# Target attention over a history of 200 tokens: the TensorE program as a loop of 96 batches, softmax and context per pair of groups

## The reference

```python
def _L0_rec_ref(target_item, history_sequence, mask, W_q, W_k, W_v, W_o):
    q = (target_item @ W_q).reshape(b, H, HD)
    k = (history_sequence @ W_k).reshape(b, S, H, HD)
    v = (history_sequence @ W_v).reshape(b, S, H, HD)
    scores = jnp.einsum('bhd,bshd->bhs', q, k) / SCALE
    scores = jnp.where(mask[:, None, :] == 0, NEG, scores)
    attn = jax.nn.softmax(scores, axis=-1)
    out = jnp.einsum('bhs,bshd->bhd', attn, v).reshape(b, A)
    return out @ W_o
```

## Time and profile before

| | us |
|---|---|
| median of 3 runs | 885.77 (878.54 to 888.96) |
| the profiled execution | 875.22 |
| its span | 873.4 |

### The profile page before, as it was taken

How to read it: one execution, slowest core, us unless ns; L and a number is a source line. 1 busy time by engine, 2 the same in 40 slices (tenths; PEclk the granted TensorE clock), 3 DMA queues, 4 the chain that set the end, 5 groups by cost and what they waited for, 6 DMA issues and landing times.

```text
span 873.4 us, 43392 instructions
## 1 busy us (share of the span) xinstructions
PE 598.9 (69%) x20451; PEld 442.2 (51%) x20451; DVE 507.5 (58%) x385; ACT 284.6 (33%) x971; POOL 27.2 (3%) x62
## 2 busy tenths in 40 slices
PE   4567667667667686667776677776676767757675
PEld 2345445446445464545554555554554545545454
DVE  4945567555665547575455774657565465774630
ACT  2312333233342233431333323333431333333233
POOL 2000000000000000000000000000000000000000
PEclk9998998998888888797988988989879897998987
DMA  8956677576876657787566885758785577875700
GB/s 351 415 173 248 273 279 311 181 274 229 309 276 223 257 219 290 277 296 271 198 246 264 307 309 190 294 203 310 277 310 223 203 263 276 312 288 204 287 17 6
DMA packets 45042, 221.42 MB, mean 254 GB/s; under 512 B 5184, under 2 KB 11840, under 8 KB 44864
## 3 DMA queue, kind: packets, MB, share of 16 engines
q1 hardware_dynamic: 44352, 217.60, 65.4%
q0 software_dynamic: 512, 1.05, 0.3%
HBM read 217.58 MB, written 1.05 MB: 250 GB/s over the span
## 4 chain that ended last, share of the span: by engine, by line
PE 54%; issue 21%; ACT 10%; DMA 9%; DVE 4%; POOL 1%; SPq 0%; ACTq 0%; DVEq 0%; POOLq 0%
PE ps_c L279 27%; PE ps_s L246 23%; DMA out<-out_sb 8%; ACT p_pad L389 6%; ACT probs L379 3%; DVE blocks L452 3%; PE ps_m L304 1%; PE ps_y L294 1%; DMA w_in<-L_rec_W_o 1%; ACT ctx_t L408 1%; PE ps_p L261 1%; POOL neg_score L188 1%; DVE probs_t L469 1%; PE ps_y L311 0%; PE ps_u L220 0%
## 5 line engine op out<-in xcount | busy, mean ns | idle before, releaser
L452 DVE STREAM_TRANSPOSE blocks<-hist 128x1664 f32<-128x1664 f32 (+1 forms) x256 | 452.3, 1814 | 224.6 <-PE ps_s L246 217.7
L279 PE MATMUL ps_c<-hist,p_pad 64*32 64x128 f32 x12800 | 251.2, 301 | 145.9 <-issue 109.5
L279 PEld LDWEIGHTS ps_c<-hist,p_pad 64*32 64x32 f32 x12800 | 211.6, 116 | 187.1 <-issue 144.6
L246 PE MATMUL ps_s<-blocks,u_pad 128*32 128x200 f32 x4096 | 248.8, 395 | 30.9 <-DVE blocks L452 22.1
L246 PEld LDWEIGHTS ps_s<-blocks,u_pad 128*32 128x32 f32 x4096 | 145.3, 129 | 111.9 <-DVE blocks L452 33.0
L389 ACT ACTIVATE p_pad<-ps_p,own 128x192 f32<-128x192 f32 (+1 forms) x512 | 166.3, 480 | 33.0 <-PE ps_p L261 33.0
L397 ACT COPY inv_ctx<-ps_y 128x2 f32<-128x2 f32 x32 | 5.1, 160 | 334.4 <-PE ps_y L294 334.4
L261 PE MATMUL ps_p<-probs_t,place_sel 128*32 128x112 f32 x1024 | 37.9, 298 | 70.5 <-DVE probs_t L469 70.5
L461 DVE COPY_PREDICATED neg_score<-mask,ps_s 128x400 f32<-128x400 int32 x32 | 19.6, 614 | 105.7 <-PE ps_s L246 105.7
L261 PEld LDWEIGHTS ps_p<-probs_t,place_sel 128*32 128x32 f32 x1024 | 28.1, 123 | 78.1 <-DVE probs_t L469 78.1
L408 ACT COPY ctx_t<-ps_m 128x128 f32<-128x128 f32 x64 | 19.1, 399 | 90.2 <-PE ps_m L304 90.2
(11 more groups left out here) (44 smaller groups left out, 98.2 us busy)
## 6 DMA issues: line engine op xcount, KB each, us to landing
hist<-r_history_sequence SPq DMA_DIRECT2D x128, 832.0 KB, 8.3
hist<-r_history_sequence SPq DMA_DIRECT2D x128, 768.0 KB, 10.1
mask<-r_mask SPq DMA_DIRECT2D x32, 200.0 KB, 8.5
x_sb<-r_target_item SPq DMA_DIRECT2D x16, 64.0 KB, 4.2
out<-out_sb POOLq DMA_DIRECT2D x16, 64.0 KB, 5.6
w_in<-L_rec_W_q SPq DMA_DIRECT2D x1, 64.0 KB, 1.9
w_in<-L_rec_W_k SPq DMA_DIRECT2D x1, 64.0 KB, 2.0
w_in<-L_rec_W_v SPq DMA_DIRECT2D x1, 64.0 KB, 8.2
```

The lines of the kernel that those rows point to most:

```text
L246: mm = pe.matmul(ps_s[s % 2][Q * b:Q * b + Q, i1 * S:(i1 + 1) * S].rearrange("p (t j) -> p t j", j=J), u_pad[s % 2][:, i, b, c, :], blocks ...
L279: mm = pe.matmul(ps_c[alpha][Q * i:Q * i + Q, 0:D], p_pad[rows, t, i, :], hist[(s * GROUPS + i) % SLOTS][rows, t, :], start=(t == 0), stop ...
L452: dve.transpose(blocks[g % 2][:, t0:t1].rearrange("p t c k -> p (t c k)"), hist[g % SLOTS][:, t0:t1, :].rearrange("p t d -> p (t d)"),).th ...
```

## The change

The unit of softmax and context is now a pair of groups, 32 batches; there are NP = 64 pairs, and a round is RING = 3 pairs, 96 batches, so 22 rounds, the last of one pair. PE runs pairs 1 to 60 as a hardware loop of 20 passes over three steps (`pe.Fori`); its waits in the loop compare with values computed from the loop's register. The other engines stay straight code. So that every pass uses the same buffers, `hist` has 6 slots instead of 10, and `u_pad`, `p_pad`, `ps_s`, masks and sums have three each; `blocks` has three instead of two, `neg_score` two.

With two groups only, `context` gives the other two column tiles to the tokens of other parity; `turn_context` multiplies by `par_sel`, which adds the two parts and transposes at once, into `ps_y`. `place` is 8 matmuls of 64 columns per pair instead of 16 of 32 per super. `combine` is 4 matmuls over 96 batches, ACT copies the result (`copy_combined`), and a new `replicate` of 4 matmuls per pair with the selection `rep_sel` puts it where ACT spreads it from. `expand` is one set of 8 activations for all 25 tokens. The copy of the context is a function of its own (`copy_context`), after `spread`, and the stores come once in three pairs. SP loads w_v and w_o one group earlier, and a mask per pair, 800 bytes a row where a super's had 1600. The host permutes the mask to match, as before for its layout.

The removed functions are those printed above. Of the diff, cut (lines that are only "..." mark what is left out):

```diff
-    GROUPS = 4
-    SUPER = GROUP * GROUPS
-    NS = B // SUPER
-    NG = NS * GROUPS
-    ROUND = 2 * SUPER
-    NR = B // ROUND
-    SLOTS = 10
-    HALVES = ((0, 13), (13, T))
+    PAIR = 2 * GROUP
+    NP = B // PAIR
+    RING = 3
+    SLOTS = 2 * RING
+    ROUND = RING * PAIR
+    NR = (NP + RING - 1) // RING
+    BLOCKS = 3
+    HALVES = ((0, 12), (12, T))
     TQ = 7
     NEG = 1e9
     INV_SCALE = float(HD) ** -0.5
-    assert D == P and GROUP * J == P and S == T * J and B % ROUND == 0 and GROUPS == 4
+    LOOPS = (NP - 1) // RING - 1
+    assert D == P and GROUP * J == P and S == T * J and NP == RING * (LOOPS + 1) + 1
...
+        blocks = [sb(f"blocks{n}", [P, T, 4, Q]) for n in range(BLOCKS)]
+
+        u_pad = [sb(f"u_pad{n}", [P, 2, B4, 4, Q]) for n in range(RING)]
+
+        p_pad = [sb(f"p_pad{n}", [P, T, 2, Q]) for n in range(RING)]
...
+            for p in range(NP):
+                for i in range(2):
+                    g = 2 * p + i
+                    for h, (t0, t1) in enumerate(HALVES):
+
+                        wait(sp, ctx_done, 2 * (p - RING) + h + 1)
+                        sp.dma_start(
+                            hist[g % SLOTS][:, t0:t1, :], history_v[g * P:(g + 1) * P, t0:t1, :],
+                        ).then_inc(hist_loaded[g % SLOTS][h], 16)
+                    if i == 0:
+                        wait(sp, masked, p - RING + 1)
+                        rows = mask[p * Q:(p + 1) * Q, :]
+                        sp.dma_start(mask_sb[p % RING][:, :],
+                                     rows.unsqueeze(1).broadcast_to([Q, H, S])).then_inc(mask_loaded[p % RING], 16)
+                    if p == 0 and i == 0:
+                        for n, w in ((2, w_v), (3, w_o)):
+                            sp.dma_start(w_in[:, n, :], w).then_inc(vo_loaded, 16)
...
+            for p in range(2, NP):
+                pool.wait_ge(exp_done, p - 1)
+                pool.memset(neg_score[p % 2][:, :], NEG).then_inc(filled, 1)
...
+            def combine(r):
+                pe.wait_ge(x_t_copied, r + 1)
+                for h in range(H):
+                    mm = pe.matmul(ps_u[:, h * ROUND:(h + 1) * ROUND], w_qk[:, h, :], x_t[:, :],
+                                   start=True, stop=True)
+                mm.then_inc(u_done, 1)
+
+            def replicate(p, ring, r):
+
+                pe.wait_ge(u_copied, r + 1)
+                wait(pe, u_pad_ready, p)
+                for c in range(4):
+                    mm = pe.matmul(
+                        ps_u[:, :].rearrange("p (n c h) -> p c h n", c=4, h=H)[:, c],
+                        rep_sel[:, c].rearrange("p a d -> p (a d)"),
+                        u_sb[:, :, ring * PAIR:(ring + 1) * PAIR], start=True, stop=True)
+                mm.then_inc(u_rep_done, 1)
+
+            def scores(p, ring, i):
+                pe.wait_ge(turned, 4 * p + 2 * i + 2)
+                if i == 0:
+                    pe.wait_ge(u_pad_ready, p + 1)
+                slot = (2 * ring + i) % BLOCKS
+                for c in range(4):
+                    for b in range(B4):
+                        mm = pe.matmul(
+                            ps_s[ring][Q * b:Q * b + Q, 0:S].rearrange("p (t j) -> p t j", j=J),
+                            u_pad[ring][:, i, b, c, :],
+                            blocks[slot][:, :, c, J * b:J * b + J],
+                            start=(i == 0 and c == 0), stop=(i == 1 and c == 3),
+                        )
...
+            def place(q):
+
+                pe.wait_ge(probs_turned, q + 1)
+                wait(pe, expanded, q)
+                for x in range(4):
+                    for alpha in range(2):
+                        mm = pe.matmul(
+                            ps_p[64 * alpha:64 * alpha + 64, 0:4 * TQ * 16].rearrange(
+                                "p (q x i r) -> p x q i r", q=TQ, x=4, i=2)[:, x],
+                            place_sel[:, x].rearrange("p l b j -> p (l b j)"),
+                            probs_t[:, :, :].rearrange("p q (i l r) -> p l q i r", i=2, l=2)[:, alpha],
+                            start=True, stop=True,
+                        )
+                mm.then_inc(placed, 1)
+
+            def context(ring, half):
+                t0, t1 = HALVES[half]
+                for t in range(t0, t1, 2):
+                    for alpha in range(2):
+                        rows = slice(64 * alpha, 64 * alpha + 64)
+                        for i in range(2):
+                            for par in range(min(2, t1 - t)):
+                                at = Q * (2 * i + par)
+                                mm = pe.matmul(
+                                    ps_c[alpha][at:at + Q, 0:D],
+                                    p_pad[ring][rows, t + par, i, :],
+                                    hist[2 * ring + i][rows, t + par, :],
+                                    start=(t == 0), stop=(t + par + 2 >= T),
+                                )
+                mm.then_inc(ctx_done, 1)
...
+            def turn_context():
+                for alpha in range(2):
+                    mm = pe.matmul(ps_y[:, 64 * alpha:64 * alpha + 64], ctx_sb[:, alpha, :],
+                                   par_sel[:, :, :].rearrange("p i r -> p (i r)"), start=True, stop=True)
+                mm.then_inc(ctx_t_done, 1)
+
+            def outputs(q):
+                pe.wait_ge(ctx_t_copied, q)
+                for h in range(H):
+                    mm = pe.matmul(ps_y[0:ROUND, P:P + D], ctx_t[:, h, :], w_vo[:, h, :],
+                                   start=(h == 0), stop=(h == H - 1))
+                mm.then_inc(y_done, 1)
+
+            def step(q, ring, r, first=False, ahead=True, replicates=True, combines=True):
+
+                after = (ring + 1) % RING
+                place(q)
+                if replicates:
+                    replicate(q + 2, (ring + 2) % RING, r + (1 if ring else 0))
+                if ahead:
+                    scores(q + 1, after, 0)
+                pe.wait_ge(expanded, q + 1)
+                if not first:
+                    pe.wait_ge(ctx_scaled, 2 * q)
+                    turn_context()
+                context(ring, 0)
+                whole = ring == 0 and not first
+                if ring == 0 and combines:
+                    pe.wait_ge(u_pad_ready, q + 3)
+                    transpose_target(r + 1)
+                if whole:
+                    outputs(q)
+                if ahead:
+                    scores(q + 1, after, 1)
+                if ring == 0 and combines:
+                    combine(r + 1)
+                context(ring, 1)
+                place_inverse(q, ring, r if whole else None)
...
+            for i in range(2):
+                scores(0, 0, i)
+            step(0, 0, 0, first=True)
+            with pe.Fori(0, LOOPS) as r:
+                step(3 * r + 1, 1, r)
+                step(3 * r + 2, 2, r)
+                step(3 * r + 3, 0, r + 1)
+            step(NP - 3, 1, NR - 2)
+            step(NP - 2, 2, NR - 2, replicates=False)
+            step(NP - 1, 0, NR - 1, ahead=False, replicates=False, combines=False)
+            pe.wait_ge(ctx_scaled, 2 * NP)
+            turn_context()
+            outputs(NP)
...
+            def exponent(p):
+                act.wait_ge(max_ready, p + 1)
+                wait(act, probs_turned, p)
+                wait(act, inv_ready, p - RING + 1)
+                if p == 0:
+                    act.wait_ge(probs_zero, 1)
+                act.activation(probs[:, 0:S], neg_score[p % 2][:, :], ACT.Exp, bias=neg_max[:, 0:1],
+                               scale=-1.0, accum_out=row_sum[p % RING][:, 0:1]).then_inc(exp_done, 1)
+
+            def expand(p):
+                act.wait_ge(placed, p + 1)
+                act.wait_ge(own_ready, 1)
+                wait(act, ctx_done, 2 * (p - RING) + 2)
+                source = ps_p[:, 0:T * 16].rearrange("p (n l h) -> p l n h", l=2, h=H)
+                for k in range(8):
+                    op = act.activation(
+                        p_pad[p % RING][:, :, :, H * k:H * k + H].rearrange("p t i h -> p (t i) h"),
+                        source[:, k // 4], ACT.Copy, scale=own[:, k:k + 1])
+                op.then_inc(expanded, 1)
+
...
+            for q in range(NP):
+                exponent(q)
+                if q >= 1:
+                    finish(q - 1)
+                expand(q)
+                if q + 2 < NP:
+                    spread(q + 2)
+                if q >= 1:
+                    copy_context(q - 1)
+                if q % RING == 0 and q // RING + 1 < NR:
+                    copy_target(q // RING + 1)
+                if q % RING == 0 and q >= RING:
+                    store(q // RING - 1)
+                if q % RING == 0 and q // RING + 1 < NR:
+                    copy_combined(q // RING + 1)
+            finish(NP - 1)
+            copy_context(NP - 1)
+            store(NR - 1)
...
+            def turn(p, i, half):
+                g = 2 * p + i
```

(98 more changed lines are left out.)

321 lines of the change are left out of this document (94 added, 227 removed).

## The result

The changed kernel takes 929.1 us (median of 4 runs, 922.27 to 934.94), the kernel before 884.3 us beside it: ratio 1.051, 95% interval 1.041 to 1.061. It is slower. It lies outside the range on record, 710 to 905, and 1 us from rival A's price of 930. The profiled execution has a span of 920.1 us.

The account below looks back on a forecast made before the run. No engine was full; PE work (54%) and "issue" (21%), read as instruction fetching, led the chain. 21 + 63 x 11.4 + 14 + 1.8 = 755 us, 764 on the median's scale; range 710 to 905.

Parts of the forecast that it names:

- rival A: PE's loop: the branch finds its code gone, everything is fetched again; 14.0 us a pair, 930 us; chance 0.25.
- the part on the loop: PE's instruction fetch: if a pass is kept, some 20 packets and 3.4 us per super gone; if not, the fetches stay.
- rival B: PE's loop: code stays but for the block at the seam, one miss per pass; 12.5 us a pair, 835; chance 0.14.
- fetches inside the pass: PE's loop, code not kept: 2.4 blocks a step at 0.7 us each, 1.7 us.
- the seams: PE's backward branch, code not kept: a missed branch at the longest stall of 4.1 us every three steps, 1.4 us.
- The sum for kept code: Whole kernel with PE's pass kept in instruction memory: 11.4 us a pair, 764 us (715 to 815), chance 0.52.
- the 3% on top: Path of a pair: added to the 11.1 us sum, a little under what the same sum misses before, giving 11.4.
- PE's own work: PE's matmul work per step at full clock: 9.3 plus a third of outputs, transpose and combine, 10.1 us.
- Waits on registers: PE's 12 waits a step with up to two register operations each: 0 to 1.4 us, taken as 0.
- Replicate: PE's 4 full matmuls per pair, new work shaped like outputs: 1.16 us a step.
- The ends: Start and finish of the span: first place at 21 us, 14 us left from the last place.
- Rival C: History loads come late with six slots: 2 us a pair, 13.4, so 890 us; chance 0.09.

Follow-up runs that it names:

- e6_slot_0: The changed kernel without a hint, the first instruction of its loop put on slot 0 of a 256-instruction block: 858.0 us, ratio 0.969 to the kernel before.
- e2_hint: The changed kernel with a prefetch hint for the backward branch, one more instruction at the head of each pass: 744.3 us, ratio 0.848 to the kernel before.

## Why the prediction was wrong

**The step that failed** is in the part on the loop: "If PE's instruction memory keeps a pass, q8 falls to some 20 packets and the 3.4 us per super are gone." The sum of 11.4 us a pair took this outcome and has no term for instruction fetches. The pass was not kept: 188 packets came, PE stood 69.4 us at the 19 returns and 59.6 us ahead of context matmuls, the clock was 0.90 and not full, and a pair took 13.92 us. Both outcomes were priced, 764 and 930, and the chance was put on the first, 0.52 against 0.25. What spoke for it was size alone, a body below what I took for the room. The count that decides was within reach: 1,860 instructions laid over blocks touch eight at the least, and the fetch runs one block ahead, as I read the earlier trace rows, so past the branch as well. Eight and one is nine. How many blocks are kept, the trace of before could not tell; but the argument had no slack for a block ahead, and rival B, "the code stays but for the block at the seam", had the ninth block and missed what it sets off. One block too many does not cost one block, it costs all. Rival B's miss of one or two blocks in a pass is seen only in some passes of `e6_slot_0`, and not in the changed kernel.

**Rival A's numbers** held, by luck in part: 14.0 us a pair was priced, 13.92 measured, but its terms missed in both directions. PE's work with the clock was put at 10.9 and is 11.4 (669.44 us of the 816 us window); fetches inside the pass at 1.7, and PE stood 0.95 (59.6 us in 63 pairs); the seams at 1.4, and they are 1.1 (69.4 us, 3.65 each where 4.1 was taken); waits for probs_t and p_pad at nothing, and they are 0.4. The fetches were put at 0.7 us a block, from before. Straight against hinted code gives (862.0 - 744.3) us for 152 - 17 = 135 packets, 0.87 us a block (0.82), clock and all.

**The sum for kept code** can be checked on `e2_hint`, which is what it described, at 764 against 744.3 measured. From 25.10 to 722.02 the place matmuls are 11.06 us apart, against a bare sum of 11.1; the 3% on top (11.4) were not there. That suggests that the 4% which the same sum had missed before belonged to fetching; it was not measured apart. By parts, predicted and in the rows above: place to turn of the context 3.8 and 3.82 (413.63 to 417.45); turn and context 2.03 and 2.11; scores to the next place 1.45 + 3.3 and 1.5 + 3.1 (419.56, 421.05, 424.14). PE's own work, put at 10.1, is 10.2 (607.02 us of the 656 us window below). The granted clock in the middle is 1.00, as was taken:

```profile
44.00:700.00 656.00, 607.02 (x17934) 485.24 (x17930) 478.00 (x478) 327.71 (x1128) 25.80 (x80) 1.00 0.87 309
```

Waits on registers were taken at 0 and bounded at 1.4 us a pair; nothing of that size is seen. Replicate, put at 1.16, is 1.16.

**The ends** were too short: the first place at 24.7 us where 21 was said, because scores waited for w_vo until 17.05 and ran at the lower clock (4.63 us for the 64 records, where 2.9 was taken); from the last place to the end of the hinted kernel's span 18.4 us (722.02 to 740.4) where 14 was said: the last context's first half ran at the 1.2 GHz level (2.81 us for 96 records, granted clock 0.50 from 726 to 731), and the `outputs` of the round before stood between its halves (1.96 us).

**Rival C** did not come: DVE waited 6.2 us for history in all, four times, with six slots, as before with ten (6.8 us, three times), and the median from issue to landing fell from 10.1 us to 6.2 us. In the hinted kernel the data queue holds the DMA engines 82% busy, and still DVE waits 6.3 us for it in all, four times.

**The range** was cut where it hurt: it left out A's upper three quarters for being improbable, when nothing in the rows made them so. A fork that no row decides should have been in the range on both sides, or the chance been nearer to even.

## What to carry to other kernels

Count a loop's body in blocks of the instruction memory, from the slot where it begins, and add the one fetched past the branch: with 256-instruction blocks on PE here, eight in all were kept and nine meant that every block was fetched again, wherever the ninth was fetched (in `e6_slot_0` it was not in some passes: 116 packets). A hint on the backward branch takes the added block away (929 to 744 us with one instruction), and where a body did not fit, straight code was the better one here (862 against 929). Look at the packets of the instruction queue first: if they do not fall when code turns into a loop, the loop has brought nothing but its branch.

## What the hardware showed that I had not expected

- PE keeps more than the one block ahead that straight code shows: bodies touching up to eight blocks of 256 instructions were fetched once with the hint, up to seven without (7 packets in 8 passes), and bodies of one more were fetched whole in every pass (70 or 71), but for `e6_slot_0`. The Trainium skill ("Runtime: NRT & Kernel Launch", Instruction fetch mechanics) gives PE 2,048 instructions and a memory replaced first in, first out, and also says that only two pages are held. These runs agree with the 2,048; with first in, first out they agree as far as they can tell; with two held pages, for PE, they do not: 880 instructions, over three blocks, ran 8 passes on 3 packets.
- A loop of 1,760 small matmul instructions takes 112 us for 8 passes when kept (102.5 busy and 9.6 idle) and 238 us (132.4 and 105.7) when it lies 128 slots further on.
- A hint does not save a body of nine blocks: 1036 us on slot 232, with stalls of 3.1 and 4.6 us in one pass's first 16 matmul records, against 929 for the body of the changed kernel without a hint and where it happened to lie.
- The granted clock rose from 0.90 to 1.00 over the middle of the span with the hint alone. PE stood for up to 3.9 us at a time without it, and for under 1 us in the step shown of the hinted kernel.
